# Cross attention: ScalarE's copies one exponential earlier, projections in steps without value matmuls, the residual two batches back

## What is computed

```python
x = x + tanh(g_xattn[0]) * cross_attention(layernorm(x), ctx_1024, ctx_1024, mask, Wq, bq, Wk, bk, Wv, bv, Wo, bo)
x = x + tanh(g_ffn[0]) * ffn(layernorm(x), q_w, k_w, v_w, o_w, sel_v_w, sel_o_w, route_scale)
```

## Time and profile before

| | |
|---|---|
| median of 3 runs | 2054.14 us (2052.46 to 2054.36) |
| profiled execution | 2055.4 us |
| its span | 2053.6 us |
| TensorE, VectorE, ScalarE, GpSimd busy | 93%, 73%, 56%, 45% |
| granted TensorE clock, mean | 0.975 |

### The profile page before, as it was taken

How to read it: one execution, slowest core, us unless ns; L and a number is a source line. 1 busy time by engine, 2 the same in 40 slices (tenths; PEclk the granted TensorE clock), 3 DMA queues, 4 the chain that set the end, 5 groups by cost and what they waited for, 6 DMA issues and landing times. The chain is left out here.

```text
span 2053.6 us, 59326 instructions
## 1 busy us (share of the span) xinstructions
PE 1916.2 (93%) x13454; PEld 1163.7 (57%) x13454; DVE 1497.0 (73%) x4285; ACT 1143.3 (56%) x3588; POOL 933.5 (45%) x1361
## 2 busy tenths in 40 slices
PE   5698999999988799999999999968999999999998
PEld 2477777777777555544444444436555555555553
DVE  6477777777777796255555555555999999999989
ACT  3477777777777644444444444434555555555543
POOL 3011121122111200266666666653766666777767
PEclk9899999999999899999999999987999999999999
DMA  3666665676666158300000000025222222222201
GB/s 115 114 106 97 103 108 99 104 102 105 106 101 89 51 223 322 128 26 26 26 26 26 26 26 26 26 91 165 79 73 76 72 76 72 76 75 70 84 14 64
DMA packets 192129, 173.99 MB, mean 85 GB/s; under 512 B 51921, under 2 KB 183378, under 8 KB 190034
## 3 DMA queue, kind: packets, MB, share of 16 engines
q1 hardware_dynamic: 189906, 165.06, 34.5%
q0 software_dynamic: 2176, 8.39, 1.2%
HBM read 112.41 MB, written 60.98 MB: 84 GB/s over the span
## 5 line engine op out<-in xcount | busy, mean ns | idle before, releaser
L1315 POOL TENSOR_TENSOR o_side<-o_side,o_tmp 128x256 f32 (+1 forms) x528 | 397.7, 753 | 192.2 <-POOL o_side L1315 73.2
L593 ACT ACTIVATE c_ex<-c_sm,c_nmax 100x361 f32<-100x361 f32 x512 | 303.9, 594 | 157.7 <-DVE c_nmax L486 136.5
L1041 ACT ACTIVATE big<-e_pv,gates 128x128 f32<-128x128 f32 x800 | 228.7, 368 | 291.4 <-PE e_pv L1103 290.1
L486 DVE CUSTOM_DVE_ANT_0 c_sm<-c_ps,c_mbias 100x361 f32<-100x361 f32 x512 | 270.3, 528 | 137.7 <-PE c_ps L665 135.8
L1436 ACT ACTIVATE o_tmp<-o_py,gates 128x256 f32<-128x256 f32 x528 | 222.3, 474 | 190.6 <-PE o_py L1509 140.8
L1103 PE MATMUL e_pv<-e_vhi,e_xhi 128*128 x800 | 303.2, 379 | 1.2 <-ACT e_out L1031 1.2
L1509 PE MATMUL o_py<-o_whi,a_chi 128*128 128x512 f16 x800 | 303.9, 380 | 0.1
L979 DVE TENSOR_SCALAR e_acc<-e_pv,gates 128x128 f32<-128x128 f32 x400 | 122.0, 347 | 249.1 <-PE e_pv L1103 249.1
L1103 PE MATMUL e_pv<-e_vlo,e_xhi 128*128 x800 | 303.2, 379 | 0.0
L1103 PE MATMUL e_pv<-e_vhi,e_xlo 128*128 x800 | 303.2, 379 | 0.0
L1509 PE MATMUL o_py<-o_wlo,a_chi 128*128 128x512 f16 x800 | 303.2, 379 | 0.0
(11 more groups left out here) (166 smaller groups left out, 3397.4 us busy)
## 6 DMA issues: line engine op xcount, KB each, us to landing
qk<-e_out SPq DMA_DIRECT2D x16, 1600.0 KB, 5.2
c_kst<-k_parts SPq DMA_DIRECT2D x256, 90.2 KB, 4.9
v<-e_out SPq DMA_DIRECT2D x20, 640.0 KB, 3.3
a_q<-qk SPq DMA_DIRECT2D x64, 200.0 KB, 2.4
a_k<-qk SPq DMA_DIRECT2D x64, 200.0 KB, 2.5
a_v<-v SPq DMA_DIRECT2D x64, 200.0 KB
c_ctx<-in_ctx_t SPq DMA_DIRECT2D x32, 361.0 KB, 3.2
e_wst<-in_v_w POOLq DMA_DIRECT2D x8, 1024.0 KB, 6.7
```

Of the source, the lines that this page charges most:

```text
L486: dve.tensor_tensor_reduce(out=sm[:, h % 4, :], in0=p_s[0:SQ, h % 2, 0:SK], in1=mbias[:, b.par, :], scale=-0.25 / WS, scalar=BIG, op0=ALU. ...
L593: act.activation(ex[:, h % 4, 0:SK], sm[:, h % 4, :], ACT.Exp, scale=-1.0, bias=nmax[:, h % 4:h % 4 + 1], accum_out=den[:, b.par, HEAD[h]: ...
L1041: act.activation(tmp[:, hh, e, :], p_v[:, hh, 1, e * PD:(e + 1) * PD], ACT.Copy, scale=gate).then_inc(s_av, 1)
L1315: pool.tensor_tensor(side[:, x.t, :], side[:, x.t, :], tmp[:, slot(x, r), j, :], ALU.add).then_inc(s_pool, 1)
```

## The change

Four things are edited in `stage_cross`. ScalarE's copies get a lag of their own, 3 instead of 4, so that the copy of head i-3 stands ahead of the exponential of head i. On VectorE the residual, moments, mean_var and keep of a batch move from steps 12 to 15 of the batch after it to steps 0 to 3 of the batch after that (`two_back`), each behind that step's masked scores. On TensorE the value matmuls of steps 8, 9 and 12 go to 9, 10 and 11, ScalarE's second value copy from step 10 to 11, and the projection from steps 10 and 11 to 14 and 15. After the last batch the calls for the batch before it are added. The streams of SyncE and GpSimd are not edited.

```diff
--- before.py
+++ after.py
@@ -298,7 +298,7 @@
-    LAG_T, LAG_C, LAG_A = 3, 4, 5
+    LAG_T, LAG_C, LAG_E, LAG_A = 3, 4, 3, 5
     RING = 2 * CLOSE
     RT = 256
     ACT_COPIES = (1, 4, 7, 10, 13, 15)
@@ -309,6 +309,11 @@
             work(b, i - lag)
         elif i < lag and not is_first(b):
             work(b.before(), i - lag + XH)
+    def two_back(b, work):
+        if not is_first(b) and not is_first(b.before()):
+            work(b.before().before())
     with ExitStack() as ctx:
         m = Store(nc, ctx)
@@ -548,19 +553,23 @@
                             rden_spread(b.before())
                         if i == 7 and not is_first(b):
                             normalize(b.before())
-                        if i == 12 and not is_first(b):
-                            residual(b.before())
-                        if i == 13 and not is_first(b):
-                            moments(b.before())
-                        if i == 14 and not is_first(b):
-                            mean_var(b.before())
-                        if i == 15 and not is_first(b):
-                            keep(b.before())
+                        if i == 0:
+                            two_back(b, residual)
+                        if i == 1:
+                            two_back(b, moments)
+                        if i == 2:
+                            two_back(b, mean_var)
+                        if i == 3:
+                            two_back(b, keep)
                 batches(dve, body)
                 last = fixed(NB - 1)
+                residual(last.before())
+                moments(last.before())
                 for i in range(XH, XH + LAG_C):
                     lagging(last, i, LAG_C, copy_ext)
+                mean_var(last.before())
+                keep(last.before())
                 rden_spread(last)
                 normalize(last)
                 residual(last)
@@ -614,19 +623,19 @@
                 def body(b):
                     for i in range(XH):
-                        lagging(b, i, LAG_C, copy_ext)
+                        lagging(b, i, LAG_E, copy_ext)
                         if i in (2, 4) and not is_last(b):
                             key_hi(b.next(), i // 2 - 1)
                         if i == 6 and not is_first(b):
                             copy_rt(b.before())
                         exp(b, i)
-                        if i in (8, 10, 14) and not is_last(b):
-                            values(b.next(), (8, 10, 14).index(i))
+                        if i in (8, 11, 14) and not is_last(b):
+                            values(b.next(), (8, 11, 14).index(i))
                 batches(act, body)
                 last = fixed(NB - 1)
-                for i in range(XH, XH + LAG_C):
-                    lagging(last, i, LAG_C, copy_ext)
+                for i in range(XH, XH + LAG_E):
+                    lagging(last, i, LAG_E, copy_ext)
                 copy_rt(last)
             @block.tensor
@@ -726,9 +735,9 @@
                 ahead = {0: (keys, 0, 0), 1: (keys, 0, 1), 2: (keys, 1, 0), 3: (keys, 1, 1),
-                         6: (values, 0, 0), 7: (values, 0, 1), 8: (values, 1, 0), 9: (values, 1, 1),
-                         12: (values, 2, 0), 13: (values, 2, 1)}
-                behind = {5: (turn_rden,), 10: (project, 0), 11: (project, 1)}
+                         6: (values, 0, 0), 7: (values, 0, 1), 9: (values, 1, 0), 10: (values, 1, 1),
+                         11: (values, 2, 0), 13: (values, 2, 1)}
+                behind = {5: (turn_rden,), 14: (project, 0), 15: (project, 1)}
                 def body(b):
                     for i in range(XH):
```

## The result

The changed kernel takes 2145.99 us (median of 4 runs, 2143.72 to 2150.01) against 2054.25 us of the kernel before in the same comparison: the ratio measured is 1.0427, 95% interval 1.0404 to 1.0451 (the quotient of the two medians is 1.0447). The forecast was 2102, from 2076 to 2131: the direction is right, the size half. The profiled execution has a span of 2148.2 us, 94.6 more than before.

A forecast was written before the change was run, and what follows sets the result against it. Bound: the key-transfer chain from a batch's first scores (S) to the next, mean period 18.74 us. Forecast: 7.90 + 2.45 + 9.81 = 20.16, + 0.25 = 20.4, +1.67 in 29 periods = +48 us, so 2102; range 2076 to 2131.

The forecast's parts named there:

- What bounds the kernel: Cross attention: 6.10 (keys computed) + 2.45 (written, landed, first read issued) + 9.81 (eight reads) = 18.36 us period.
- the residual behind S holds SyncE's queue: SyncE's store waits for the residual after a batch's first scores; 2.8 us of slack used up, 1.8 us missing.
- The chain's steps: SyncE's stream after a batch's first scores: store at 1.88, query loads 2.38, context 7.36, high key parts 7.90 us.
- the price of the context's data ahead of the high key parts: DMA: context load 0.5 us before the high key parts delays them 0.5 us, between nothing and 1.0.
- The relief of 0.25 on the reads: Stacked-key reads: store and query loads no longer mix with them, -0.25 us, between nothing and -0.55.
- Rival C: Slower by more: TensorE's idle seam drops the clock, two half-clock stretches in a row; period 21.4, +77 us, 2131; chance 0.10.
- Part (1): ScalarE's copies one exponential earlier free TensorE's transposes: 0.3 us gained on the key chain, bounds 0 and 0.5.
- the stall in step 4: TensorE's transpose stall of 0.54 us ahead of the low key parts: up to 0.5 us could come off their 7.89.
- the one in step 15: TensorE's transpose stall ending in front of the seam wait: what it gains becomes seam wait, nothing.
- Part (3): VectorE's four operations moved to steps 0 to 3: net nothing on the key chain, bounds -0.5 and +0.5.
- Part (2): TensorE's value matmuls and projections moved among steps 8 to 15: nothing, as long as the seam wait covers it.
- The fixed 2.45 us: SyncE, from high key parts to first stacked-key read: written, landed, first read issued; 2.45 us, kept unchanged.

The follow-up runs named there:

- e2: The kernel before with only VectorE's residual, moments, mean_var and keep moved two batches back: 2149.6 us, 1.037.
- e3: The changed kernel with the residual of step 0 ahead of that step's copy and masked scores instead of behind them: 2103.5 us, 1.0156.
- e4: The changed kernel with SyncE's store at the end of a body writing the batch before the last one: 2103.3 us, 1.0145.
- e15: The changed kernel with SyncE's context load ahead of the query loads and 18 small matmuls in the wait at the seam: 2112.4 us, 1.0252.
- e5: The changed kernel with SyncE's context load ahead of the eight query loads, the hold at the store kept: 2117.2 us, 1.0222.
- e11: The changed kernel, hold and all, with 24 small unused matmuls of TensorE in the wait at the seam: 2154.0 us, 1.0411.
- e8: e4 with 16 small unused matmuls of TensorE in the wait at the seam: 2068.3 us, 1.0051.
- e1: The kernel before with only ScalarE's copies one exponential earlier: 2103.0 us, 1.0209.
- e10: e4 with the high key activation ahead of the copy in ScalarE's steps 2 and 4, and 13 small matmuls in the seam: 2057.4 us, 0.9935.
- e6: e4 with ScalarE's copies back at lag 4, as in the kernel before: 2057.8 us, 0.9996.
- e12: The kernel before with ScalarE's second high key activation in step 3 instead of step 4: 2049.0 us, 0.9918.
- e13: The kernel before with the second high key activation in step 3 and the second low key part in step 4, instead of 4 and 5: 2028.2 us, 0.9851.
- e9: The kernel before with 4 small matmuls in the wait at the seam: 2052.1 us, 0.9914.

## Why the prediction was right or wrong

**What bounds the kernel** was read rightly: a chain from S over the key parts to the stacked reads, 9.8 us from first read to next S. It measured 9.5 to 10.0 in the mean of every run. That the residual behind S holds SyncE's queue was right: e2 alone makes the loss, and e3 and e4, without the hold, are 46 us faster than e2. The chain's steps came out nearly as priced: store at S+1.93 (forecast 1.88), query loads at 2.67 (2.38), context at 7.65 (7.36), in the means of the 28 batches with the hold; high parts at 8.2 (7.90) where the clock doesn't hold them up longer.

**The step that failed** is the price of the context's data ahead of the high key parts. I took 0.5 us with an upper end of 1.0, from a row in which a write ran beside other traffic. The sum had the first read at 7.90 + 2.45 + 0.5 = S+10.85; it came at S+12.31, 1.46 later, and 1.46 x 29 = 42 us is nearly all of the 44 that are missing. With the context moved away and the clock full in nearly all batches, it came at 10.92 (e15). So the context costs 12.31 - 10.92 = 1.39 us and not 0.5, most of it in the landing (3.9 us against 2.8 in e15); by e5, whose clock falls about as often as the changed kernel's, it costs 1.18. So this term was 0.9 us too small (0.7 by e5), some 26 us in 29 periods. The other 0.57 of the 1.46 (10.92 against the 7.90 + 2.45 = 10.35 of the sum) are two smaller errors: the high parts go 0.2 later than the steps of SyncE gave, and the gap behind them is 0.4 wider even without the context, for a reason that wasn't found.

I had bounded the context's price by its landing of before, 3.1 us; it now took 3.6, and the high parts came behind that. The Trainium skill's rule (DMA: Bandwidth & Descriptors, Queues, rings and completion order), that an engine takes its descriptors in ring order, pointed to the upper end, and the trace agrees with it: whether the high parts were issued at S+8.2 or S+9.2, the first read came near S+12.2. That fits data queued behind data, but no run shows the order of the packets. The relief of 0.25 on the reads was right (9.51 instead of 9.78).

**Rival C** was right about the clock and wrong about its price; that its 2131 lies nearer to the 2146 than the forecast is luck. The clock fell at nearly each seam, in half of them even for two stretches, as C had it, and the high parts were then later than C's S+8.9, at 9.2. But the first read stayed near S+12.3, behind the context's data, and e11 shows that the clock costs the changed kernel nothing that can be measured. What the Trainium skill (TensorE: Matmul & The Clock Gate, HAM oscillation) says of a DMA wait that returns the clock to 1.2 GHz at each tile holds here: without work in that wait 27 of 30 batches start cold (e4), with it none (e8), and e8 is 35 us faster, or 19 by the ratios.

**Part (1)** was wrong in sign, though this didn't count in the total. I took the stall in step 4 for a gain of 0.3 us and said of the one in step 15 that it becomes seam wait, "nothing". The copies ahead of the key activations cost 0.29 us, since the high parts' issue and not only the low parts' matters. They stand ahead of both activations (head 15 in step 2, head 1 in step 4), where I had named only the second. And the seam wait isn't nothing: without the hold it pulls the clock down in 28 of 30 batches. By e8, in which the clock is held and 35 us come back, that is most of e1's 43 us. Part (3) had 0.2 us left over of VectorE's own work, and 0.30 are left in e10. Part (2) isn't contradicted: e6 contains it and ties with before, but with a loss and a gain in it that cancel, and no run has it alone.

**The fixed 2.45 us** between high parts and first read is the later of two releases, high parts landed or low parts issued. In the kernel before the two fell so near each other that they looked like one: in e12 the high parts went 0.6 us earlier and the first read followed by only 0.1, and in e13, with the low parts earlier too, it followed by 0.5.

## What to carry to other kernels

Before moving an operation across the point where a loop's period closes, look for stores that wait for it, and for what stands behind them in the same queue: here one residual, 5.5 us later (S+13.9 before, and S+1.1 of the next batch now), held eleven loads and the key transfers behind them. When a period closes on a DMA, a stall taken out of the middle reappears in front of it (e1: 0.77 us at the seam became 2.9), and idle time gathered in one place can cost TensorE its clock: 28 of 30 batches started cold, where it was 9. Two DMAs that share the queue and come close are better priced one after the other: here 180 KB issued 0.8 us behind 361 KB took 3.9 us to land instead of 2.4, and the first read came 1.2 to 1.4 us later for it. And a fixed distance in one trace can be the later of two releases.

## What the hardware showed that was not expected

Useless matmuls made the kernel faster, by 35 us (e8 against e4; 19 by the ratios) and by 18 (e9 against before). And one program's time varied by 1% between executions with the granted clock, from 2047.5 us at 0.979 to 2068.4 at 0.970 in one group. In the profiles a cold batch takes 1.3 us longer than a full-clock one (19.65 against 18.35 in the kernel before), so 16 more of them in a run would make up those 21 us; that this is the whole reason wasn't shown.
